# Attention with relative position bias in a small vision tower: 128-row score tiles, head pairs in the two row halves of TensorE, and all other products as jobs between score steps

## The reference, cut to the part that matters

```python
h1 = _rmsnorm(x, norm1_w)
q = (h1 @ wq).reshape(b, l, H, DK)
k = (h1 @ wk).reshape(b, l, H, DK)
v = (h1 @ wv).reshape(b, l, H, DV)
basis = _rel_basis(l, N_POS)            # 32 functions of j - i
qw = jnp.einsum('bihd,hdn->bihn', q, w_pos)
qr = jnp.einsum('bihn,ijn->bhij', qw, basis)
uk = jnp.einsum('hd,bjhd->bhj', u_param, k)[:, :, None, :]
vw = jnp.einsum('hd,hdn->hn', v_param, w_pos)
vr = jnp.einsum('hn,ijn->hij', vw, basis)[None]
bias = (qr + uk + vr) * scale
scores = jnp.einsum('bihd,bjhd->bhij', q, k) * scale + bias
attn = jax.nn.softmax(scores, axis=-1)
out = jnp.einsum('bhij,bjhd->bihd', attn, v)
x = out.reshape(b, l, H * DV) @ wo + bo + skip
```

## Time and profile before

| what | us |
|---|---|
| median of 3 runs (1118.44 to 1126.41) | 1119.12 |
| the profiled execution | 1114.98 |
| its span, first to last instruction | 1113.0 |
| TensorE matmuls busy | 955.5 |
| VectorE busy | 724.7 |
| ScalarE busy | 673.7 |
| GpSimd busy | 134.6 |

### The profile page before, as it was taken

How to read it: one execution, slowest core, us unless ns; L and a number is a source line. 1 busy time by engine, 2 the same in 40 slices (tenths; PEclk the granted TensorE clock), 3 DMA queues, 4 the chain that set the end, 5 groups by cost and what they waited for, 6 DMA issues and landing times. The chain is left out here.

```text
span 1113.0 us, 20727 instructions
## 1 busy us (share of the span) xinstructions
PE 955.5 (86%) x6738; PEld 828.2 (74%) x6738; DVE 724.7 (65%) x1567; ACT 673.7 (61%) x1197; POOL 134.6 (12%) x199
## 2 busy tenths in 40 slices
PE   5999999999978978897889789967869961999993
PEld 5899999999957765776677568736836651999993
DVE  7899979799437864875487558726653354455543
ACT  5767847578248875886687568834322315557546
POOL 1000000000001440244034304420000000000000
PEclk9999999999988999899989999988989995999995
DMA  7021001399126843683377149730001113322101
GB/s 241 20 71 33 35 10 33 73 152 148 31 67 185 281 124 97 194 264 93 114 230 237 54 117 290 203 87 20 1 0 41 45 29 90 97 79 59 46 0 57
DMA packets 78721, 112.67 MB, mean 101 GB/s; under 512 B 10917, under 2 KB 38866, under 8 KB 78562
## 3 DMA queue, kind: packets, MB, share of 16 engines
q1 hardware_dynamic: 78658, 111.93, 37.4%
HBM read 61.07 MB, written 47.68 MB: 98 GB/s over the span
## 5 line engine op out<-in xcount | busy, mean ns | idle before, releaser
L417 PE MATMUL psum<-w,feat 128*128 128x192 f32 x960 | 167.8, 330 | 13.6 <-ACT feat L336 9.9
L417 PEld LDWEIGHTS psum<-w,feat 128*128 128x128 f32 x960 | 156.6, 192 | 14.5 <-issue 9.9
L803 POOL TENSOR_SCALAR a_scores<-a_scores,a_inv 112x514 f32<-112x514 f32 (+1 forms) x160 | 113.1, 707 | 291.3 <-DVE a_inv L1149 291.2
L1134 DVE CUSTOM_DVE_ANT_0 a_scores<-psum,a_bias 112x514 f32<-112x514 f32 (+1 forms) x160 | 109.8, 688 | 51.0 <-PE psum L876 42.7
L1026 ACT ACTIVATE a_scores<-a_scores,a_least 112x514 f32<-112x514 f32 (+1 forms) x160 | 116.6, 729 | 14.1 <-DVE a_least L1134 13.5
L435 PE MATMUL psum<-w_parts,parts 128*128 128x384 f32 x368 | 114.2, 375 | 2.4 <-DVE parts L228 2.3
L889 PE MATMUL psum<-ident,a_scores 112*112 112x112 f32 (+1 forms) x800 | 103.1, 261 | 14.3 <-DVE a_probsT L1144 9.3
L336 ACT ACTIVATE feat<-turn 128x1024 f32<-128x1024 f32 (+1 forms) x60 | 58.5, 974 | 87.5 <-DVE turn L211 53.8
L876 PE MATMUL psum<-a_kh,a_q 128*112 128x258 f32 (+1 forms) x320 | 103.3, 343 | 6.5 <-DVE a_q L1104 4.2
L889 PEld LDWEIGHTS psum<-ident,a_scores 112*112 112x112 f32 (+1 forms) x800 | 78.7, 137 | 34.4 <-POOL a_scores L803 16.9
L437 PE MATMUL psum<-w_parts,parts 128*128 128x192 f32 x384 | 97.3, 253 | 0.0
(11 more groups left out here) (219 smaller groups left out, 1797.5 us busy)
## 6 DMA issues: line engine op xcount, KB each, us to landing
shear<-a_pos SPq DMA_DIRECT2D x128, 224.9 KB, 3.9
a_bias<-shear SPq DMA_DIRECT2D x128, 224.4 KB, 3.9
shear<-zero SPq DMA_DIRECT2D x20, 448.9 KB, 16.6
e_fc<-in_e_fc_dram SPq DMA_DIRECT2D x8, 672.0 KB, 5.7
x<-in_xT_dram SPq DMA_DIRECT2D x20, 256.0 KB, 2.8
e_proj<-in_e_proj_dram SPq DMA_DIRECT2D x8, 576.0 KB, 6.4
shear<-a_pos SPq DMA_DIRECT2D x32, 130.5 KB
a_bias<-shear SPq DMA_DIRECT2D x32, 130.3 KB
```

The source lines that it names most:

```text
L417: mm = pe.matmul(sums[m][:, 0:D], feat[:, r, j, 0, 128 * m:128 * m + 128], w[:, k, :], start=begins, stop=ends)
L803: pool.tensor_scalar(row, row, inv[0:TILES[g % NT][1], g % TT:g % TT + 1], 1.0, ALU.mult, ALU.mult).then_inc(weighed, 1)
L1134: dve.tensor_tensor_reduce(halves(scores[0:r, g % TT, 0:PADL]), psum2(score_pair(g), r), halves(bias[0:r, g % MR, :]), -1.0 / 8, BIG, ALU. ...
```

## The change

The attention block is written anew.

- Tiles have 128 rows. The first 512 query rows of a head make four tiles, so an image has 32 tiles, and two of them (the same rows of the two heads of a pair) make a step u = 0 to 15. The 513th row of all eight heads is one extra tile of 36 rows (heads at rows 0 to 3 and 32 to 35), done once per image at step 8 to 11. The 513th key is handled apart: its probabilities are gathered by `last_keys` jobs into `lastT`, and one more matmul in `values` adds its term.
- Queries and keys of a head pair stand on 128 partitions, 64 for each head. A score is three terms, hi·hi, lo·hi and hi·lo, each a matmul with a contraction of 64 rows; the two heads of the pair alternate, head e in partitions 64e to 64e+63 and in banks 2e and 2e+1. The second copies of the keys are gone.
- A step's scores fill banks 0 to 3. Banks 4 and 5 hold positions as before, bank 6 the transposes (four of 128 columns, a whole bank), and bank 7 is free for other products. Everything that is not a score, a position or a transpose is one of 41 jobs. The table `STEPS` puts up to three in each step: one in bank 7 ("own"), one in bank 0 once the step's first tile has its bias added ("even"), one in bank 2 once the second has ("odd"). The next step's scores wait until the jobs in banks 0 and 2 have been copied out.
- Whole transposes are copied out by ScalarE for even tiles and by VectorE for odd ones; positions likewise. The images follow each other without a stretch of products: jobs of the next image ("p", and "q" and "k" of pairs 0 and 1) and of the one before (the last keys, the last values and the projection) are in the table too. The products of the first image stand ahead of it.
- The restacking of `qpos` is in two halves of 12 transfers, after the transfers of step 9 and of step 15. The ring in HBM has 16 slots of 128 rows.
- The image's input copy `h1` is made by GpSimd (in step 2), as are the small copies for the 513th row.

The core of the diff:

```diff
+    ROWS, NTILE, PAIRS = s.SROWS, N // s.SROWS, H1 // 2
+    NG, NU2 = H1 * NTILE, H1 * NTILE // 2
+    AHEAD, LAG = 8, 4
+    RT, MR, TT, RING = 4, 8, 8, s.RING
+    RW = 32 + G4
+    TERMS = (("hi", "hi"), ("lo", "hi"), ("hi", "lo"))
...
+    STEPS = [
+        (("keys", 1, 3), ("q", 2, 0), None),
+        (("values", 1, 1), ("q", 2, 1), None),
+        (("project", 0, 0), ("k", 2, 0), ("project", 0, 1)),
+        (("project", 1, 0), ("keys", 0, 0), ("project", 1, 1)),
+        (("v", 0, 2), ("v", 2, 4), ("v_last", 0, 0)),
+        (("keys", 0, 1), ("values", 0, 0), ("k", 2, 1)),
+        (("q", 3, 0), ("q", 3, 1), ("keys", 0, 2)),
+        (("k", 3, 0), ("k", 3, 1), ("row_position", 0, 0)),
+        (("p", 0, 0), None, ("p", 0, 1)),
+        (("keys", 0, 3), ("values", 0, 1), ("q", 0, 0)),
+        (("q", 0, 1), ("k", 0, 0), ("keys", 1, 0)),
+        (("k", 0, 1), ("row_values", 0, 0), ("q", 1, 0)),
+        (("q", 1, 1), None, ("keys", 1, 1)),
+        (("values", 1, 0), ("p", 1, 0), None),
+        (("p", 1, 1), ("k", 1, 0), ("keys", 1, 2)),
+        (("k", 1, 1), None, None)]
+    BANKS = (7, 0, 2)
...
+            def image(b, first, more):
+                for u in range(NU2):
+                    for g in (2 * u + AHEAD, 2 * u + AHEAD + 1):
+                        if g < NG:
+                            store(b, g, first)
+                        elif more:
+                            store(b + 1, g - NG, False)
+                        if g - LAG < NG:
+                            load(b, g - LAG, first)
+                        elif more:
+                            load(b + 1, g - LAG - NG, False)
+                    if more and u == 9:
+                        stack(b + 1, 0)
+                    if more and u == NU2 - 1:
+                        stack(b + 1, 1)
...
+            def image(b, first, more):
+                for u in range(NU2):
+                    for g in (2 * u, 2 * u + 1):
+                        pool.wait_ge(total_inv, b * NG + g + 1)
+                        stand_alone(pool, passed)
+                        pool.tensor_scalar(scores[:, g % TT, :], scores[:, g % TT, :], inv[:, g % TT:g % TT + 1], 1.0, ALU.mult,
+                                           ALU.mult).then_inc(weighed, 1)
+                    if u in (2, 5, 9):
+                        pool.wait_ge(weighed, b * NG + 2 * u + 2)
+                    if u == 2:
+                        load_image(b, first)
+                        pool.wait_ge(image_in, b + 1)
+                    if u == 5:
+                        last_positions(b, first)
+                        pool.wait_ge(row_q_set, b * 2 + 1)
+                    if u == 7:
+                        last_queries(b, first)
+                    if u == 9:
+                        pool.wait_ge(row_inv, b + 1)
+                        stand_alone(pool, passed)
+                        pool.tensor_scalar(row_scores[:, :], row_scores[:, :], row_recip[:, :], 1.0, ALU.mult, ALU.mult).then_inc(row_weighed, 1)
+                        pool.wait_ge(row_weighed, b + 1)
+                    if more and u == 9:
+                        third_part(b + 1, 0)
+                    if more and u == 14:
+                        third_part(b + 1, 1)
...
+            def last_keys(b, hg, t, bank):
+                g = hg * (NG // 2) + G4 * t
+                pe.wait_ge(weighed, b * NG + g + G4)
...
+                bank = BANK[n]
+                pe.wait_ge(job_out[bank], per_image[bank] * b + nth(n))
+                if (first and n in OF_BEFORE) or (not more and n in OF_NEXT):
...
+                if bank != 7:
+                    pe.wait_ge(biased, b * NG + 2 * AT[n] + (1 if bank == 0 else 2))
+                run(b, b + (n in OF_NEXT) - (n in OF_BEFORE), n)
...
+            def score(b, u, first):
+                p, i0 = pair_of(u), ROWS * tile_of(2 * u)
+                if u or not first:
+                    pe.wait_ge(biased, b * NG + 2 * u)
+                if u == 9:
+                    pe.wait_ge(row_biased, b + 1)
+                made = [job for job in STEPS[u - 1][1:] if job] if u else []
+                if u % (2 * NTILE) < 2 and (p >= 2 or not first):
+                    made += [(kind, p, w, -(p < 2)) for kind in "qk" for w in range(2)]
+                wait_out(b, *made)
+                for w in range(2):
+                    for n, (q_part, k_part) in enumerate(TERMS):
+                        for e in range(2):
+                            rows = slice(DK1 * e, DK1 * e + DK1)
+                            mm = pe.matmul(s.bank[2 * e + w][:, 0:HALF + 1], q[q_part][rows, p, i0:i0 + ROWS],
+                                           k[k_part][rows, p, w * HALF:w * HALF + HALF + 1], start=n == 0, stop=n == 2)
+                            if w == 1 and n == 2:
+                                mm.then_inc(scores_done, 1)
...
+            def flip_row(b):
+                pe.wait_ge(row_weighed, b + 1)
+                pe.wait_ge(put_d, b * (NG // 2) + 9)
+                stand_alone(pe, passed)
...
+                score(b, u, first)
+                if u == 10:
+                    flip_row(b)
+                job(b, in_own, first, more)
+                behind(2 * u - 2)
+                ahead(2 * u + AHEAD)
+                job(b, in_even, first, more)
+                job(b, in_odd, first, more)
+                ahead(2 * u + AHEAD + 1)
+                behind(2 * u - 1)
+                if u == 8:
+                    score_row(b)
...
+            def take(b, i, count, hi_count, kind, a, w, bank, first):
+
+                act.wait_ge(job_done, count)
+                if kind == "p":
+                    if not first:
+                        act.wait_ge(stacked[a], 16 * 3 * G4 * i)
+                    act.copy(parts[:, a, 0, window(w)], s.bank[bank][:, 0:HALF]).then_inc(hi_done, 1)
+                    if w:
+                        act.wait_ge(rest1, i * 4 + a * 2 + 2)
+                        act.copy(parts[:, a, 1, :], rest[:, :]).then_inc(part2, 1)
+                else:
+                    if not first:
+                        last = 2 * NTILE * (a // 2) + 2 * NTILE - 2 + a % 2
+                        act.wait_ge(scores_done, i * NG - NG + 2 * last + 2)
+                        act.wait_ge(row_scored, i)
+                    dst = (q if kind == "q" else k)["hi"]
+                    act.copy(dst[:, a, window(w)], s.bank[bank][:, 0:HALF]).then_inc(hi_done, 1)
...
+            def step(b, u, first, more):
+                in_own, in_even, in_odd = jobs_at(u)
+                if u == 10:
+                    put_row(b)
+                weigh(b, 2 * u)
+                job(b, in_own, first, more)
+                if 2 * u + AHEAD < NG:
+                    position_out(b, 2 * u + AHEAD, first)
+                elif more:
+                    position_out(b + 1, 2 * u + AHEAD - NG, False)
+                if u:
+                    put(b, 2 * u - 2, first)
+                elif not first:
+                    put(b - 1, NG - 2, False)
+                job(b, in_even, first, more)
+                job(b, in_odd, first, more)
+                weigh(b, 2 * u + 1)
+                if u == 8:
+                    weigh_row(b)
+
...
+            def step(b, u, first, more):
+                in_own, in_even, in_odd = jobs_at(u)
+                add_bias(b, 2 * u, first)
+                add_bias(b, 2 * u + 1, first)
+                if u:
+                    invert(b, 2 * u - 1)
+                elif not first:
+                    invert(b - 1, NG - 1)
+                if u == 9:
+                    dve.wait_ge(row_exp, b + 1)
+                    dve.reciprocal(row_recip[:, :], row_total[:, :]).then_inc(row_inv, 1)
+                job(b, in_own, first, more)
+                invert(b, 2 * u)
+                job(b, in_even, first, more)
+                job(b, in_odd, first, more)
+                if 2 * u + AHEAD + 1 < NG:
+                    position_out(b, 2 * u + AHEAD + 1, first)
+                elif more:
+                    position_out(b + 1, 2 * u + AHEAD + 1 - NG, False)
+                if u:
+                    put(b, 2 * u - 1, first)
+                elif not first:
+                    put(b - 1, NG - 1, False)
+                if u == 8:
+                    add_bias_row(b, first)
...
-        s.RING, s.PITCH = 20, 2 * L
-        s.shear = nc.dram_tensor("shear", [s.RING, TILE + 1, s.PITCH], F32).ap()
+        s.RING, s.PITCH, s.SROWS = 16, 2 * L, 128
+        s.shear = nc.dram_tensor("shear", [s.RING, s.SROWS + 1, s.PITCH], F32).ap()
```

866 lines of the change are left out of this document (449 added, 417 removed).

## The result

The change makes the kernel slower: 1158.94 us in the median of 4 runs (1155.59 to 1161.36) against 1118.78 for the kernel before, beside it on the same chip. The ratio is 1.034, with a 95% interval of 1.029 to 1.039. The forecast was 1075, with a range of 1040 to 1110.

The account below looks back on a forecast made before the run. No engine was taken as full before; after the change, one chain per step bounds it. First bias at 336.3, four images of 89, plus 4, minus 9, plus 6 gave 693.3 against 737.7: 44 us less, 1075, range 1040 to 1110.

Parts of the forecast that it names:

- From one image to the next no engine is full.: Attention block before the change: time goes into products that stand alone and into waits; a middle image lasts 105.6 us.
- rival 3: Attention block: TensorE's clock falls to 1.2 GHz; at half the time there, 57 us more, 1132; chance 0.1.
- the waits of steps 0 and 10: Waits for tile 31 of the image before and the 513th row's tile; steps of 6.1 and 7.8 us.
- A job of two takes 0.43: TensorE's price for a product job of two 257-column matmuls: 0.43 us, usable 0.17 later.
- The score matmuls: Each step's 12 matmuls of 64 rows: 0.96 us, between 0.72 (halves at once) and 1.44 (one after the other).
- Rival 1: Score matmuls: row halves don't run at once, each step 0.5 us longer, 32 us more, 1107; chance 0.2.
- score starts 0.12 apart: Sign in the score matmuls that the forecast is wrong and the row halves don't run at once; right was 0.05 to 0.1.
- The work of the 513th row and key: TensorE: 24 matmuls, 2.9 us, in step 8; 34 one-column matmuls, at most 2 us, in step 11.
- stall some 1.5: First restacking half: tile 24's load lands late, a stall of some 1.5 us in three images, 4 us.
- rival 2: SyncE's restacking is not hidden: 26 us more, 1101; chance 0.1.
- The chain through ScalarE and VectorE: Each step: scores, bias, exponential, four copies and subtraction run as one chain, 5.1 us for a full step.
- Rival 4: VectorE bounds: engines overlap better, 4.3 us an ordinary step, 44 us less again, 1031; chance 0.14.

Follow-up runs that it names:

- inverse_between: restack_early with VectorE's inverse of the previous step's odd tile put between the two bias additions; 1106.6 us, ratio 0.986, the fastest of all.
- restack_early_half: restack_early with every q, k and position product made from one of its two contraction chunks; 1125.3 us, ratio 1.000.
- the fillers: The changed kernel with 20 unread matmuls ahead of each of the waits in steps 0 and 10; 1168.9 us, ratio 1.040.
- waits_off_spread: The changed kernel with 513th-row transposes a step later, last keys job in step 0's odd place, GpSimd's small copies earlier, restacking in threes; 1137.8 us, ratio 1.017.
- row_tile_later: The changed kernel with the 513th row's transposes and their copy moved from step 10 to step 11; 1159.9 us, ratio 1.033.
- restack_spread: The changed kernel with the 24 restacking transfers sent three at a time instead of in two blocks of 12; 1166.2 us, ratio 1.042.
- restack_early: The changed kernel with reordered GpSimd work, keys job and value sums, and the first restacking half in two groups of six from step 9; 1115.3 us, ratio 0.991.
- thin_row: The changed kernel with 22 of the 24 score matmuls of the 513th row's tile left out; 1152.7 us, ratio 1.030.
- halves_in_turn: The changed kernel with each step's score matmuls ordered by head instead of alternating between the two heads; 1161.4 us, ratio 1.036.
- three_waits_off: The changed kernel with 513th-row transposes a step later, last keys job in step 0's odd place, first restacking half a step later; 1143.5 us, ratio 1.018.

## Why the prediction was wrong, point by point

**"From one image to the next no engine is full."** This step failed first. I argued it with VectorE's and ScalarE's shares in the earlier trace rows and left TensorE's 19.7 of 24 us and 39.6 of 46 out of the conclusion, though I used the same 82 to 86% against rival 3. TensorE had 92.8 us of work in an image of 105.6. I never added up TensorE's work for one image of the change. The only figure I had for it stands in rival 3: 3.5 us a step, 56 an image. It is 86.4 us at the high clock (inverse_between), 5.4 a step, so an image of 89 would have wanted TensorE 97% busy, where the best order found here reached 91%.

This is not the whole miss of 84 us. The second part is the waits and the clock behind them: I priced the waits of steps 0 and 10 too low, that of the restacking at 1.5 us, and the clock at nothing. Changes of order that leave out no work bring the kernel from 1158.9 to 1106.6, so 52 us of the miss are waits and clock, and it is these that make the change slower than the kernel before. The remaining 32 us, from 1106.6 to 1075, I put down to TensorE's work. That rests on the busy share alone, in which the ends of matmuls are modelled: the one run with less work in a late order, restack_early_half, met a late load, and none took work away in the best order.

**The price of a product.** "A job of two takes 0.43": in the earlier trace rows I read the four matmuls in 1.03 us as two jobs, since a job is two calls in the code. The trace has two matmul instructions for each call in float32, and the row is one job: 0.86 us on the engine. Twenty of them an image: 8.6 us missed. The value sum was put at 1.1 us and the value rows at no more than an ordinary step; measured in step 5:

```profile
479.52 1.93 PE L945 MATMUL psum<-a_probsT,a_v 128*32 128x256 f32 x32 [0.76 <-DVE a_least L1323]
481.38 0.70 PE L947 MATMUL psum<-a_lastT,a_v_last 36*128 36x256 f32 x2
```

That is 2.5 us, and the three jobs of value rows hold TensorE 4.7 us in step 4. With the wait of 0.8 to 0.9 us for the keys job in steps 5 and 9, these are the 1.6 to 2.4 us by which steps 1, 4, 5 and 9 are longer than forecast, 7.9 in all. Steps 2, 3, 6, 7, 14 and 15 were within 0.1 to 0.8.

**The score matmuls** (0.96, bounds 0.72 to 1.44) came out at the lower bound: pairs start 0.12 us apart, six pairs in 0.72 us, so the row halves run at once. Rival 1 is out. From step 5 of the change:

```profile
484.30 0.29 PE L1049 MATMUL psum<-a_k_hi,a_q_lo 64*128 64x258 f32 x2
484.42 0.28 PE L1049 MATMUL psum<-a_k_lo,a_q_hi 64*128 64x258 f32 x2
```

My sign for it, "score starts 0.12 apart", was ill put: 0.12 is the distance of pairs. The Trainium skill, "TensorE: Matmul & The Clock Gate", section on packing small matmuls, says that different row groups run at the same time; the trace agrees, with pairs 0.12 us apart, as single matmuls are in the earlier trace rows.

**The work of the 513th row and key** was taken as 2.9 us in step 8 and "at most 2 us" in step 11. By the groups of lines in image 1 of the change, its matmuls are busy 15.6 us (L1062 5.1, L935 3.4, L947 2.8, and 4.3 in five smaller groups). By the same measure the scores, transposes and positions of all other tiles fell from 90.6 to 64.0 us. (Such groups overlap one another, so their sums are above the engine's busy time.) More than half of what the larger tiles save went back into one row and one key.

**The waits of steps 0 and 10** were seen, in kind and place: forecast 6.1 and 7.8, measured 8.4 and 10.5. What I left out is the clock behind them, 1.6 us each in image 1 by the fillers, 0.2 to 1.6 in the others.

**Restacking: "stall some 1.5", and rival 2.** The forecast had the block end 11.2 into step 10; it ended 13.6 in (526.8), since the third part came at 516.8 + 1.1, 4.6 into the step where I had 3.4. The place was right and the price too small: steps 11 to 13 took 22.9 us for 15.15 forecast, with the clock at 0.64 in step 12. Rival 2 was the nearest of my rivals, but I gave it 0.1 and priced it without what waits behind the late bias: inverse, scaling, keys job, and all of TensorE behind that.

**Rival 3, the clock.** It was 0.92 between 392 and 728 us, where it had been 0.97, and not under 0.8. I had it as a consequence of a low busy share everywhere. It came at single waits of 2.8 to 3.9 us instead. In image 1 TensorE was busy 92.3 us where the same work takes 86.4 at a clock of 1.00: some 6 us an image, not 115 in the block.

**The chain through ScalarE and VectorE**, my "main point", holds at most in a few steps: taking 0.37 us off each exponential gained 3 us in all. Rival 4, VectorE as the bound at over 85% busy, is out by VectorE's 66.5 us in an image of 111.8.

So: TensorE's work is 92 us an image as before (at a lower clock; it would be 86.4), what the other engines lost was never the bound, and the new order adds waits that feed one another. With the waits taken out by moves alone, the same work runs in 1106.6, where the mechanism of the change does pay, with a third of the gain that I forecast. My floor of 96 us an image and 1115 in all, given with waits_off_spread, was wrong too: it took the 92 us, part of which are at the low clock. What is still left: 2 us of a late load in step 12, and the 1.26 us in which TensorE stands ahead of the scores of step 9. The trace calls them "issue", but the code waits there for `row_biased`, and VectorE adds the 513th row's bias from 503.36 to 504.05 us; the scores start at 504.25. This wait was in the forecast of step 8.

## What to carry to other kernels

Before any chain of latencies is added up, sum each engine's own work for one period, from the rows of the trace and instruction by instruction, and compare it with the forecast period; here one such sum (86 to 92 us, against a forecast image of 89) would have stopped the forecast. Count instructions in the trace, not calls in the code. Where one wait is removed and nothing is gained, look one step later before the theory is dropped: row_tile_later and restack_spread gained nothing alone, and all the moves together 52 us. On an engine that runs in order, whatever stands behind a tile of the next step waits for the next step, even if that engine is busy only 11% of the time.

## What the hardware showed that I had not expected

Half of the products less did not make any of three kernels faster. In the kernel before, the same stretch at the start ran at a granted clock of 0.50 and took 6.98 us for 7.20; in restack_early a late load took the gain, and over half of the 10 us lost is not explained. It is no rule: thin_row, with 22 matmuls of the 513th row less, gained 6 us. Matmuls without a use, in a wait of 3.6 us, gave back 1.6 us of clock behind it in image 1.

At the turn of the image loop, from image 1 to 2, two of the kernels show a stretch in which hardly any engine works. In the run with fillers TensorE idles 5.4 us, "issue" meaning that nothing which the profile shows held it:

```profile
555.00:560.00 5.00, 0.00 (x0) 0.00 (x0) 0.37 (x1) 0.00 (x0) 0.18 (x1) 0.54 0.68 192
```

```profile
560.04 0.58 PE L1051 MATMUL psum<-a_k_hi,a_q_hi 64*128 64x258 f32 x2 [5.40 <-issue]
```

The changed kernel with half products has 4.9 us there and another 1.8 in the midst of the scores behind it, the change itself 0.2. It is the place where the queues jump back; what causes it no run here tested. The last step of 7.4 us instead of 5.1 in halves_in_turn and row_tile_later is another thing: TensorE is busy 6.4 of 7.4 us in halves_in_turn, at a granted clock of 0.50, and three_waits_off has such a step in image 0, where no queue jumps back:

```profile
554.15:561.56 7.41, 6.36 (x28) 4.29 (x28) 3.27 (x10) 2.98 (x7) 2.51 (x3) 0.50 0.54 165
```

```profile
435.33:442.79 7.46, 6.78 (x30) 4.78 (x31) 3.27 (x10) 2.98 (x7) 2.51 (x3) 0.50 0.62 146
```
